# Turning the normalised rows of a batch by VectorE and sixteen DMAs instead of TensorE

## The reference, cut to what matters

```python
x = _layernorm(x + attention(x, Wq, Wk, Wv, Wo, bo))     # "x1": 8 x 512 x 128, float32
logits = einsum('bsh,eh->bse', x, gate_w) + expert_bias  # needs x1 with the channels on the partitions
weights = softmax(logits); top_w, top_i = top_k(weights, 2)
for e in range(8):
    h = gelu(x @ w_up[e].T); out += sparse_w[..., e:e+1] * (h @ w_down[e].T)
x = _layernorm(x + (_layernorm(out) + x))
```

## Time and profile before

| | |
|---|---|
| median of 3 runs | 832.34 us |
| profiled execution, its own time | 833.57 us |
| its span (first to last instruction) | 831.8 us |
| granted TensorE clock over the span | 0.996 of full |
| TensorE busy | 808.2 us, 97% |
| VectorE busy | 676.2 us, 81% |
| ScalarE busy | 623.1 us, 75% |
| GpSimd busy | 554.5 us, 67% |
| chain that ended last, share of TensorE | 92% |

### The profile page before, as it was taken

How to read it: one execution, slowest core, us unless ns; L and a number is a source line. 1 busy time by engine, 2 the same in 40 slices (tenths; PEclk the granted TensorE clock), 3 DMA queues, 4 the chain that set the end, 5 groups by cost and what they waited for, 6 DMA issues and landing times.

```text
span 831.8 us, 21102 instructions
## 1 busy us (share of the span) xinstructions
PE 808.2 (97%) x6267; PEld 591.3 (71%) x6267; DVE 676.2 (81%) x2711; ACT 623.1 (75%) x1672; POOL 554.5 (67%) x612
## 2 busy tenths in 40 slices
PE   8999999999999999999999999999999889999995
PEld 4566666666666666666666666666666569999995
DVE  6887798889888988898889988988898856225996
ACT  4677787888788878887887778777877766555576
POOL 5765646456756775667568866775687236899893
PEclk9999999999999999999999999999999999999999
DMA  5111101000100010001001100100012246424435
GB/s 164 33 40 40 52 20 33 8 20 27 52 14 27 27 39 15 29 27 36 17 27 31 36 18 23 41 25 15 14 47 83 61 130 205 132 82 127 129 113 156
DMA packets 55438, 46.09 MB, mean 55 GB/s; under 512 B 6368, under 2 KB 47072, under 8 KB 55328
## 3 DMA queue, kind: packets, MB, share of 16 engines
q1 hardware_dynamic: 50960, 35.90, 15.1%
q0 software_dynamic: 4224, 8.72, 3.1%
q10 hardware_dynamic: 144, 0.13, 0.1%
HBM read 28.39 MB, written 12.14 MB: 49 GB/s over the span
## 4 chain that ended last, share of the span: by engine, by line
PE 92%; DVE 3%; issue 2%; ACT 1%; DMA 1%; POOL 0%; another core or an unknown queue 0%; SPq 0%; DVEq 0%; ACTq 0%
PE TB L1026 18%; PE S_all L979 18%; PE TB L1010 14%; PE S_all L1177 7%; PE AO L1047 7%; PE TB L1190 4%; PE AO L1190 4%; PE S_all L1010 3%; PE AO L908 3%; PE AO L906 3%; PE AO L907 3%; PE AO L970 1%; PE AO L968 1%; PE AO L969 1%; PE AO L903 1%
## 5 line engine op out<-in xcount | busy, mean ns | idle before, releaser
L1295 ACT ACTIVATE Pr_all<-Sm,nmax 128x512 f32<-128x512 f32 (+3 forms) x512 | 280.6, 554 | 0.0
L1504 DVE CUSTOM_DVE_ANT_0 Sm<-S_all,causal 128x512 f32<-128x512 f32 (+3 forms) x512 | 220.1, 486 | 66.6 <-PE S_all L979 66.5
L665 POOL TENSOR_TENSOR shared<-shared,sin_t 128x512 f32<-128x512 f32 x63 | 80.3, 1275 | 168.5 <-DVE shared L1484 168.3
L1307 ACT ACTIVATE PT<-TB 128x1024 f32<-128x1024 f32 x185 | 131.0, 742 | 63.8 <-PE TB L1010 63.5
L979 PE MATMUL S_all<-kT,qT 64*128 64x512 f32 (+3 forms) x1024 | 166.7, 443 | 1.9 <-POOL kT L668 0.9
L1026 PE MATMUL TB<-PT,shared 128*64 128x128 f32 x1008 | 151.2, 441 | 5.3 <-ACT PT L1307 0.3
L1525 DVE SCALAR_TENSOR_TENSOR x_acc<-AO,rinv,x_acc 128x128 f32<-128x128 f32 x504 | 141.7, 344 | 4.1 <-remote 1.9
L1010 PEld LDWEIGHTS TB<-ident,Pr_all 128*128 128x128 f32 x1000 | 108.0, 141 | 38.3 <-ACT Pr_all L1295 21.1
L1010 PE MATMUL TB<-ident,Pr_all 128*128 128x128 f32 x1000 | 133.7, 277 | 0.5 <-ACT PT L1307 0.5
L979 PEld LDWEIGHTS S_all<-kT,qT 64*128 64x128 f32 x1024 | 78.9, 187 | 71.2 <-issue 54.4
L1026 PEld LDWEIGHTS TB<-PT,shared 128*64 128x64 f32 x1008 | 69.9, 137 | 58.3 <-issue 39.4
(11 more groups left out here) (320 smaller groups left out, 1418.4 us busy)
## 6 DMA issues: line engine op xcount, KB each, us to landing
wo<-in_wo SPq DMA_DIRECT2D x64, 64.0 KB, 1.8
PT<-yrows SPq DMA_DIRECT2D x7, 512.0 KB
w_tile<-in_wup SPq DMA_DIRECT2D x10, 256.0 KB
xt<-xrows SPq DMA_DIRECT2D x32, 65.0 KB
x_acc<-in_x SPq DMA_DIRECT2D x8, 256.0 KB
wdown<-in_wdown SPq DMA_DIRECT2D x8, 256.0 KB, 3.2
pay<-pay SPq DMA_DIRECT2D x8, 256.0 KB
x_acc<-pay SPq DMA_DIRECT2D x8, 256.0 KB
```

The source lines that it names most:

```text
L665: nc.gpsimd.tensor_tensor(k_rot, k_rot, sin_t[:, :], ALU.mult).then_inc(k_mul, 1)
L1295: nc.scalar.activation(Pr[j][:, 0:n], Sm[j], ACT.Exp, bias=nmax[:, j:j + 1], scale=-1.0, accum_out=rsum[p][:, h * QB + qb:h * QB + qb + 1] ...
L1307: last = nc.scalar.activation(PT[p][:, :, 0:qb + 1, qb * P:qb * P + P], source, ACT.Copy)
L1504: nc.vector.tensor_tensor_reduce(out=Sm[j], in0=SB[2 * (group % 2) + h][:, at:at + n], in1=causal[:, T - n:T], scale=-0.125, scalar=HUGE, ...
```

## The change

The four blocks of every batch but the last are no longer turned by TensorE. At the head of the unit of pair 3 VectorE transposes each 32x32 square of `pay` in place of its position (`turn_x1`, one instruction of 128 partitions and 512 elements) into `xT_all`, the memory of the four `xT` tiles, which only the experts' part used. A square of tokens 32q and channels 32c then still lies in the partitions of its tokens. Sixteen DMAs on SyncE's queue (`move_squares`), one for each pair (q, c), take it to the partitions of its channels in `x1T`. SyncE issues them after the transposition, once the logits of the batch before are done, and ahead of `copy_rows`. The logits wait for all sixteen (`x1T_in`). TensorE's wait for the copy (L1122) goes. For the last batch the old way stays. A semaphore that nobody waited for (`eps_set`) goes too.

```diff
-        xT = [sb(f"xT{i}", [P, P]) for i in range(4)]
+        xT_all = sb("xT_all", [P, 4, P])
+        xT = [xT_all[:, i, :] for i in range(4)]
+        x1_turned = xT_all[:, :, :].rearrange("p c (i t) -> p c i t", t=SQ)
...
                 if n == TURN_AT and batch > 0:
+                    move_squares(batch - 1)
                     copy_rows(batch - 1)
...
+            def move_squares(b):
+                sp.wait_ge(x1_square, b + 1)
+                wait(sp, logits_done, b)
+                for tokens in range(SQUARES):
+                    for channels in range(SQUARES):
+                        sp.dma_start(x1T[channels * SQ:channels * SQ + SQ, :].rearrange("c (i q t) -> c q i t", i=QB, q=SQUARES)[:, tokens, :, :],
+                                     x1_turned[tokens * SQ:tokens * SQ + SQ, channels, :, :]).then_inc(x1T_in, 16)
...
             def logits(b, u):
-                pe.wait_ge(x1T_ready, b + 1)
+                if b < B - 1:
+                    pe.wait_ge(x1T_in, 16 * SQUARES * SQUARES * (b + 1))
+                else:
+                    pe.wait_ge(x1T_ready, 1)
...
-                if batch > 0 and n == TURN_AT + 1:
-
-                    pe.wait_ge(x1T_ready, batch)
...
-                if batch > 0 and n == TURN_AT:
-                    transpose_x1(batch - 1, u)
...
+            def turn_x1(b):
+                dve.wait_ge(x1_ready, (QB + 1) * (b + 1))
+                wait(dve, x1T_in, 16 * SQUARES * SQUARES * b)
+                nc.vector.transpose(x1_turned.rearrange("p c i t -> p i c t"),
+                                    pay[b % 2][:, :, 0, 0:C].rearrange("p i (c t) -> p i c t", t=SQ)).then_inc(x1_square, 1)
...
+                if batch > 0 and n == TURN_AT:
+                    turn_x1(batch - 1)
                 mask_max(u, 0)
                 mask_max(u, 1)
...
-                    if n == TURN_AT:
-                        copy_x1T(batch - 1)
```

More of the change, by code:

```diff
@@ L30 @@
 VS = 4
+SQ = 32
+SQUARES = P // SQ
 VBLOCKS = B * PAIRS // VS * QB
@@ L341, in build_block @@
         chain = sem("chain")
-        eps_set = sem("eps_set")
         direct_ready = sem("direct_ready")
@@ L350, in build_block @@
         x1_tr, x1T_ready = sem("x1_tr"), sem("x1T_ready")
+        x1_square, x1T_in = sem("x1_square"), sem("x1T_in")
         logits_done = sem("logits_done")
@@ L1176, in up @@
                 for ib in range(IB):
-                    last = nc.tensor.matmul(HB[t % 3][:, ib * P:ib * P + P], w_tile[t % AHEAD][:, ib * P:ib * P + P], xT[t % 4][:, :],
+                    last = nc.tensor.matmul(HB[t % 3][:, ib * P:ib * P + P], w_tile[t % AHEAD][:, ib * P:ib * P + P], xT[t % 4],
                                             start=True, stop=True)
@@ L1350, in copy_xT @@
                 act.wait_ge(x_tr, t + 1)
-                nc.scalar.activation(xT[t % 4][:, :], XB[t % 2], ACT.Copy).then_inc(xT_ready, 1)
+                nc.scalar.activation(xT[t % 4], XB[t % 2], ACT.Copy).then_inc(xT_ready, 1)
             def gelu(t):
@@ L1580, in copy_x1T @@
             def copy_x1T(b):
-                dve.wait_ge(x1_tr, b + 1)
+                dve.wait_ge(x1_tr, 1)
                 nc.vector.tensor_copy(x1T[:, :], route_bank(b)[:, :]).then_inc(x1T_ready, 1)
+            def turn_x1(b):
[3 more added lines that the diff above has]
+                                    pay[b % 2][:, :, 0, 0:C].rearrange("p i (c t) -> p i c t", t=SQ)).then_inc(x1_square, 1)
             def read_logits(b):
@@ L1744, in attention @@
                     for dst, eps in ((eps_t, LN_EPS), (eps_sum, 4 * LN_EPS), (eps_half, LN_EPS / 4)):
-                        nc.vector.memset(dst[:, :], eps).then_inc(eps_set, 1)
+                        nc.vector.memset(dst[:, :], eps)
                     dve.wait_ge(pool_set, POOL_SET)
+                if batch > 0 and n == TURN_AT:
+                    turn_x1(batch - 1)
                 mask_max(u, 0)
```

## The result

The changed kernel takes 844.91 us (median of 4 runs, 842.84 to 846.0), the one before 833.12 in the same comparison. The ratio is 1.0145, 95% interval 1.013 to 1.016: 11.8 us slower where 5.6 had been forecast, and 0.4 above the upper end of the range, 844.5. The profiled execution has a span of 843.5 us for 831.8.

The account below looks back on a forecast made before the run. TensorE was taken to bound the attention. Stall less gain, six times 0.67 (4.0 us) plus 1.6 in the fifth batch, gave 5.6 us on 832.34: 838.0 us, range 834.5 to 844.5.

Parts of the forecast that it names:

- the head of the unit of pair 3: VectorE waits for GpSimd's copy, then transposes, delaying masks; TensorE loses net 0.67 us a batch, 1.77 in the fifth.
- The estimate from the Trainium skill: VectorE transposition at pair 3's head: 1.24 us instead of 0.63, which would make the sum 4.3 us higher.
- Rival 3: At pair 3's head the transposition waits for GpSimd's multiplication: 1.13 us more a batch, 845.9 us in all; chance 8 in 100.
- the gain: TensorE drops four transpositions in each of seven batches: 0.24 us a batch, or 0.43 with nothing swallowed.
- I count nothing and keep 0 to 2.6: Seventh batch: sixteen square transfers need 9.0 us, logits come after 9.75; in time, or TensorE stands 2.6 us once.
- The step from one issue to the next: SyncE's spacing of the sixteen square transfers: 0.45 us taken, range 0.38 to 0.66.
- the upper bound of 12.4: Longest time in us allowed for the sixteen square transfers, from first issue to last landing; 9.0 was taken.
- nothing is late next: In the unit of pair 4, after pair 3's stall, VectorE reaches the next rope at about the old time; no further loss.

Follow-up runs that it names:

- wait_only: Kernel before, plus only VectorE's wait for x1_ready at the head of the unit of pair 3; 834.0 us, ratio 1.0043.
- turn_only: Kernel before, plus a VectorE transposition of a constant at the head of pair 3, no wait, result unused; 829.78 us, ratio 0.9994.
- turn_late: Changed kernel with the VectorE transposition moved behind the eight masks; 862.67 us, ratio 1.0415 to the kernel before.
- no_turn: Kernel before without turning the rows of the first seven batches, nothing in their place; 829.76 us, ratio 0.9995.
- issue_forms: Kernel before, plus four extra transfers after copy_rows in each unit of pair 3, another form each batch; 830.51 us beside 830.32.
- split_later: Changed kernel, but in unit 44 GpSimd makes x_lo after the rotations of k and q; 842.53 us, one run.
- squares_first: Changed kernel, seventh batch's square transfers issued ahead of the expert-weight load and last-mask wait; 835.74 us, ratio 1.0067 to the kernel before.
- logits_last: Changed kernel, transposition between masks 5 and 6, squares ahead of weight loads, logits at pair 4's end; 832.97 us, ratio 1.0032 to the kernel before.

## Why the prediction was wrong

**Right: the head of the unit of pair 3.** Forecast 0.67 a batch and 1.77 in the fifth, measured 0.63 and 1.73. wait_only, turn_only and turn_late show each part. The times of the steps, 124.60 and 125.23, were met to the hundredth, and that is partly luck: the unit began 0.09 later than before, and VectorE started 0.03 after GpSimd's copy and not 0.10. Counted from the unit's start, mask 0 was 0.96 late for 1.05, the third score group 0.73 for 0.86, and the stall of the whole unit 0.87 (0.63 + 0.24) for 0.91. The estimate from the Trainium skill weighed there, 1.24 us from four times 311 ns ("VectorE: DVE Perf Modes", "The three transpose paths"), is not borne out for the one instruction of 32-bit numbers: it took 0.71 us, 0.63 from start to start. Rival 3 is out as well: the transposition took 0.71 us in all seven batches, 0.06 to 0.08 behind the start of GpSimd's multiplication, with no wait of 1.13 in it, and the multiplication 1.26 to 1.28 us. By the Trainium skill ("SBUF — State Buffer", "Who interferes with whom") a VectorE instruction with one SBUF input outside the two-port modes keeps clear of GpSimd, and the trace agrees.

**Right: the gain.** 0.24 us a batch and not 0.43 (turn_late, no_turn).

**Wrong: the DMAs in the seventh batch, "I count nothing and keep 0 to 2.6".** It cost 5.0 us. By the forecast's own terms the squares are late there from (9.75 - 1.8) / 16 = 0.50 us a step on, inside its range of 0.38 to 0.66, so the nothing hung on the choice of 0.45. Three things failed in that step:
- The step from one issue to the next. I took 0.45, "nearer the row with as many runs"; it is 0.65. The rows held both candidates, and the number of runs was the wrong thing to match: `wo` comes from HBM, while L523, the row I set aside as the bound, goes from SBUF to SBUF like the squares. issue_forms shows that this is what counts. Sixteen times 0.20 is 3.2 us, of which the slack of 0.75 swallows a part: 2.4 us late by this alone, near the 2.6 of the upper bound.
- Single long issues. One of the sixteen took 1.82 us, 1.2 more than the rest, which even the upper bound of 12.4 didn't hold: from the first issue to the last landing it took 13.1 (the last issue starts at 642.9 and the logits follow at 644.76, so 1.9 from there, for a forecast of 1.8). That makes the logits 3.3 late.
- The lower clock after TensorE's wait: 1.7 us, and 3.3 in split_later. I priced waits by their length alone.

squares_first takes all of it back at once and lands on 5.6 us, which makes the seventh batch the cause of the miss. The 0.4 us above the range is no more than the 0.8 by which the kernel before came out higher in the comparison (833.12) than where the forecast stood (832.34); the loss itself is twice the one forecast.

**Wrong by 0.55: "nothing is late next".** That was said of pair 4, but in the fifth batch GpSimd's lateness moved its two-operand work beside VectorE's subtraction L1621, which stood 1.64 us, and TensorE lost 0.55 us in unit 45. It had been held before the change too, 0.80 us, at no cost. That the one made the other is likely and not proven (split_later). By the Trainium skill ("SBUF — State Buffer", "Who interferes with whom") a VectorE instruction with two SBUF inputs contends with a GpSimd instruction that reads SBUF, and whoever issues first blocks the other. The trace agrees as to the blocking (1.64 and 0.85 us for 0.19, ending with GpSimd's), and in logits_last as to the order. It doesn't as to the order in unit 44, where the row of the blocked one starts 0.29 us earlier.

Of the remaining 0.8 us 0.6 lies behind the start of the last unit (173.0 us for 172.4); its cause is open.

## What to carry to other kernels

A wait and a piece of work that each fit into an engine's idle time may not fit together: add them, and compare the sum with the idle time plus the slack of whoever is behind. When many small DMAs replace one instruction, price the issuing queue first, with the row of a transfer between the same two memories, and look at what else that queue waits for in every unit, not only in the typical one. And before an exchange, leave the old work out once: here the most to be won was 0.2% by the units, and in the whole time it couldn't be told from nothing.

## What the runs showed of the hardware

- An issue on SyncE with SBUF on both sides takes 0.60 us whatever the partitions (32 or 128) and runs (one or four), with HBM on one side 0.42 to 0.5 (issue_forms) and 0.33 for `wo`. In 24 of the 49 series of sixteen one issue took 1.0 to 1.8. What makes it long stays open.
- A VectorE 32x32 transposition of 128x512 f32 takes 0.66 to 0.71 us, and 1.13 when it writes with a step of 16 bytes. A load of TensorE's weights with such a step took 0.33 for 0.19 and made the unit of the eight logits matmuls 0.97 longer.
- After waits of 2.2 to 3.4 us TensorE's clock fell to 1.2 GHz in some cases and not in others of nearly the same length: 16.44 us for the unit with a wait of 2.20, 13.42 for the one with 2.32; 15.84 with 3.17 and 17.43 with 3.09. What decides it isn't shown.
- A VectorE subtraction of 128x32 with both operands in SBUF took 0.85, 1.64 and 1.90 us for 0.19 beside GpSimd's two-operand work (logits_last, the changed kernel, wait_only). A VectorE transposition beside it was not held.
